# A different hand-over of the last pair of sequences to the router and to the first expert tile, in an attention and mixture-of-experts kernel

## The chip, the cores and the metric

The kernel runs on one core of a Trainium2 chip. The metric is the device time of one execution in microseconds (us). Each kernel is timed in several runs, and the median is given with the lowest and the highest. Durations of single instructions come from one execution under the hardware profiler.

## What is computed

Sixteen sequences of 100 tokens with 256 features go through two layers:

```python
x = x + cross_attention(layernorm(x), ctx)      # 16 heads of 16, rotary positions, window of 64 keys back
xf = layernorm(x).reshape(1600, 256)
probs = softmax(xf @ router_w.T)                # 8 experts
topk_p, topk_i = top_k(probs, 2); topk_p /= topk_p.sum(-1)
for e in range(8):
    mask = (topk_i == e).any(-1)
    mean_w = (topk_p * (topk_i == e)).sum() / mask.sum()     # one weight for each expert
    out += mask * ((silu(xf @ gate_e.T) * (xf @ up_e.T)) @ down_e.T) * mean_w
x = x + out
```

An expert works only on the tokens that chose it. Its products are made from numbers split in a high part (TensorE's rounded fp32 format, fp32r) and a low part (what is left), three products for one: high by high, low by high, high by low.

## The kernel before, in words

**Attention.** The 16 sequences are worked off as NPAIR = 8 pairs. Each engine has its own hand-written program with a loop `for i in range(-1, NPAIR + 2)` over pairs and inside it `for n in range(8)` over quarters of heads. At (i, n) it does pair i's attention, prepares pair i + 1, finishes pair i - 1 (output projection, residual) and routes pair i - 2. The order of instructions on an engine is the order in this text; semaphores (`s_...`) tie the engines together. Nothing is planned at run time.

**Routing of a pair i - 2.** VectorE: `residual` (L997) adds the attention output to x and takes mean and variance (`norm_stats`, s_var2). POOL: `inverse_deviation` (L1235) makes rstd2. VectorE: `rows_write` (L1006) writes the normalized rows and their token numbers into `xrow` (s_xr). TensorE: `x2_transpose` (L547) turns them; ACT: `x2_copy` (L772) copies them; TensorE: `route_logits` (L557); VectorE: `choose` (L1016) takes the best of 8, `choose_masks` (L1028) and `choose_counts` (L1037) build `sel`, `chosen` and the running counts `before` (s_ch), `top_differences` (L1077) the difference of the two best logits (s_dl). TensorE: `ranks` (L567) sums how many earlier tokens chose each expert. VectorE: `places` (L1043), `destinations` (L1050) make the row numbers in `slots`, a DRAM array with a region for each expert. POOL: `scatter` (L1267) sends the rows there, four indirect DMAs a pair. ACT: `top_exponentials` (L779); POOL: `weight_sums` (L1249), seven small operations, adds the weights of the experts up (s_wpair).

**The first tile of expert 0.** An expert tile has 448 tokens. Tile 0 does not wait for the last two pairs' scatters. SP loads what is in `slots` into `xin` early (L382), TensorE transposes it into two banks (`early_tile`, L586), and the rows of pairs 6 and 7 that belong to expert 0 are added there by products with a matrix of ones and zeros (`late_rows`, L594). That needs the high and low part of the rows (`rows_high` on ACT, L785; `rows_low` on VectorE, L1061) and the matrix `onehot`: `hot_columns` (L1066) compares the slot numbers with the token's own (`here`), one column block for each sequence. After the last pair TensorE sums the counts (L664) and the weights (L669). `warm` (L581) issues products whose result nobody reads.

**The experts.** In `block` (L709) TensorE runs eight steps f: `hidden` (L681), 12 products for gate and up, and from f = 3 on `project_down` (L695) of step f - 3. At f = 7, before `hidden`, it transposes the next tile out of `xin` (`tile_transpose`, L673). ACT and VectorE follow it in their `step` functions (L873, L1191). In a step VectorE does `gated` (silu times up), waits for ACT's `hidden_high`, does `hidden_low`, and in the first tile of an expert also `weights_low`, which waits for ACT's `weights_high`; these split the next expert's weights.

**The tokens' numbers.** Each row in `xin` carries its token number. `take_ids` (L1177) copies them to `idnext`, once `xin` has landed (s_in), and adds to s_id. There is one `xin`. SP (L405 to L411) loads tile t when tile t's turn of s_xt (transposes of tile t - 1 done) and of s_id (numbers of tile t - 1 taken) has come; both start with a credit of one. Tile 0 is so loaded a second time, whole, after all scatters, for its numbers alone. With e == 0, `take_ids(0)` stands at f == FC - 5 = 3, and `take_ids(t + 1)` at f == FC - 2 = 6:

```python
for f in range(FC):                 # VectorE, L1193
    gated(t, f)
    hidden_low(t, f)
    if split and f < WCH:           # WCH = 6
        weights_low(e, par, f)
    if e == 0 and split and f == FC - 5:
        take_ids(0)
```

## Time and profile before

| what | value |
|---|---|
| median of 3 runs | 486.79 us (485.64 to 487.36) |
| the profiled execution, its own time | 483.92 us |
| its span in the trace | 482.1 us |
| TensorE busy in the span | 446.3 us (93%) |
| VectorE, ACT, POOL busy | 301.0, 272.6, 142.0 us |
| mean granted clock of TensorE | 0.982 |
| expert tiles | 8, one for each expert |

The span is what the trace covers; the own time of that execution is 1.8 us longer. Attention takes about the first 200 us of the span, routing of the last two pairs the next 15, the experts the rest. PE is TensorE, PEld its weight loads, DVE is VectorE, ACT is ScalarE, POOL is GpSimd, SP issues DMAs. PEclk is the granted clock, 1.00 for 2.4 GHz and 0.50 for 1.2 GHz. An idle time in square brackets is the engine's wait ahead of that instruction, with what ended it.

### The profile page before, as it was taken

Reading aid. Unit: us, or ns where it says so; the run is one execution under the profiler, and the core shown is the slowest. Engines: PE = TensorE matmul, PEld = TensorE weight load, DVE = VectorE, ACT = ScalarE, POOL = GpSimd, SP = SyncE. Lnnn points to the kernel's source line nnn. Section 1 sums busy time; section 2 is a strip of 40 time slices with the busy share of each in tenths; the row PEclk is TensorE's granted clock in tenths of the full one; section 3 lists DMA queues with packets and bytes.
Section 4 is the critical chain, followed back from the end, with each engine's and each line's share of the span. In section 5 each row is a group of like instructions: output and inputs, shape, how many; then the busy total and the mean of one; then the engine's idle time right before and its main releaser. Section 6 shows DMA issues by size and latency. Waiting matters only on the chain.

```text
span 482.1 us, 8983 instructions
## 1 busy us (share of the span) xinstructions
PE 446.3 (93%) x2787; PEld 367.9 (76%) x2787; DVE 301.0 (62%) x735; ACT 272.6 (57%) x863; POOL 142.0 (29%) x174
## 2 busy tenths in 40 slices
PE   3898999999999999889999999999999999999980
PEld 2655666757565655569899999999999999999980
DVE  2565769898979878775737647466465473763330
ACT  1286887878788888335445545455464554554230
POOL 5111013544446262673023050140410502205013
PEclk9999999999999999989999999999999999999995
DMA  8173421111202020229956545565465553213002
GB/s 229 41 210 111 175 78 33 39 41 33 67 6 67 8 63 26 84 76 384 300 151 155 180 78 170 166 125 164 111 164 154 89 170 94 27 40 41 0 5 34
DMA packets 24588, 50.48 MB, mean 105 GB/s; under 512 B 5410, under 2 KB 15302, under 8 KB 24394
## 3 DMA queue, kind: packets, MB, share of 16 engines
q10 hardware_dynamic: 7886, 26.44, 17.6%
q1 hardware_dynamic: 10508, 16.47, 11.3%
q0 software_dynamic: 6144, 6.97, 8.8%
q8 instruction: 23, 0.38, 0.3%
q14 instruction: 27, 0.22, 0.2%
HBM read 39.62 MB, written 13.20 MB: 110 GB/s over the span
## 4 chain that ended last, share of the span: by engine, by line
PE 69%; DVE 7%; ACT 7%; DMA 5%; issue 5%; POOL 3%; ACTq 1%; POOLq 0%; SPq 0%; DVEq 0%
PE b_o L703 9%; PE b_small L703 8%; PE b_s L690 7%; PE b_s L692 7%; PE b_s L691 7%; PE b_s L445 6%; ACT probs L831 4%; PE b_pv L468 3%; PE b_proj L523 3%; PE b_pt L454 3%; PE b_pt L690 2%; PE b_pt L692 2%; PE b_pt L691 2%; PE b_proj L499 2%; DMA xin<-slots 2%
## 5 line engine op out<-in xcount | busy, mean ns | idle before, releaser
L831 ACT ACTIVATE probs<-b_s,negmax 100x100 f32<-100x100 f32 x256 | 85.4, 359 | 24.1 <-DVE negmax L1108 16.7
L1320 POOL DMA_INDIRECT out<-y_sb,idnow x32 | 49.7, 1552 | 158.7 <-ACT y_sb L869 151.4
L857 ACT CAST h_hi<-h_sb 128x448 fp32r<-128x448 f32 x64 | 36.3, 567 | 88.1 <-DVE h_sb L1185 88.1
L690 PE MATMUL b_s<-x_hi,w_hi 128*128 128x448 f32 x192 | 71.5, 372 | 0.0
L692 PE MATMUL b_s<-x_hi,w_lo 128*128 128x448 f32 x192 | 70.4, 367 | 0.0
L691 PE MATMUL b_s<-x_lo,w_hi 128*128 128x448 f32 x192 | 70.0, 364 | 0.0
L1086 DVE TENSOR_TENSOR w_lo<-w_raw,w_hi 128x1024 fp32r<-128x1024 f32 x48 | 58.8, 1225 | 13.8 <-ACT w_hi L792 13.4
L1189 DVE TENSOR_TENSOR h_lo<-h_sb,h_hi 128x448 fp32r<-128x448 f32 x64 | 40.0, 625 | 40.5 <-ACT h_hi L857 39.9
L831 ACT ACTIVATION_READ_ACCUMULATOR probs<-b_s,negmax 100x1 f32 x256 | 56.5, 221 | 0.0
L445 PE MATMUL b_s<-kblk,qrot 128*100 128x400 f32 x128 | 53.7, 500 | 0.0
L792 ACT CAST w_hi<-w_raw 128x1024 fp32r<-128x1024 f32 x48 | 50.4, 1050 | 0.0
L1108 DVE TENSOR_REDUCE negmax<-b_s 100x4 f32<-100x400 f32 x64 | 36.2, 566 | 20.6 <-PE b_s L445 20.2
L1185 DVE TENSOR_TENSOR h_sb<-b_s,act 128x448 f32<-128x448 f32 x32 | 19.9, 620 | 43.7 <-PE b_s L692 39.8
L853 ACT ACTIVATE act<-b_s 128x448 f32<-128x448 f32 x64 | 34.4, 538 | 17.4 <-PE b_s L692 17.4
L692 PEld LDWEIGHTS b_s<-x_hi,w_lo 128*128 128x128 f32 x192 | 36.5, 190 | 2.9
L1274 POOL DMA_INDIRECT slots<-xrow,desti x32 | 34.3, 1072 | 14.7 <-issue 7.3
L691 PEld LDWEIGHTS b_s<-x_lo,w_hi 128*128 128x128 f32 x192 | 36.6, 191 | 2.2
L690 PEld LDWEIGHTS b_s<-x_hi,w_hi 128*128 128x128 f32 x192 | 36.6, 191 | 1.9
L454 PEld LDWEIGHTS b_pt<-cst,probs 100*100 100x100 f32 x256 | 26.2, 128 | 14.8 <-issue 14.2
L703 PE MATMUL b_small<-w_lo,h_hi 128*112 128x256 f32 x128 | 35.9, 281 | 0.0
L703 PE MATMUL b_o<-w_hi,h_lo 128*112 128x256 f32 x128 | 35.9, 280 | 0.0
L703 PE MATMUL b_small<-w_hi,h_lo 128*112 128x256 f32 x128 | 35.9, 280 | 0.0
(153 smaller groups left out, 969.5 us busy)
## 6 DMA issues: line engine op xcount, KB each, us to landing
w_raw<-in_ffw ACTq DMA_DIRECT2D x48, 512.0 KB, 3.9
xin<-slots SPq DMA_DIRECT2D x10, 449.8 KB, 4.4
slots<-in_padrows SPq DMA_DIRECT2D x9, 449.8 KB, 4.1
kblk<-krot SPq DMA_DIRECT2D x128, 12.5 KB
out<-x_all SPq DMA_DIRECT2D x8, 200.0 KB
ctx_all<-in_ctxT SPq DMA_DIRECT2D x1, 1200.0 KB, 6.5
x_all<-in_x SPq DMA_DIRECT2D x1, 1200.0 KB
attw<-in_wT ACTq DMA_DIRECT2D x2, 256.0 KB, 3.9
```

Source lines behind the costliest of these rows:

```text
L445: pe.matmul(o, qrot[:, i % 2, 2 * c + b, :], kblk[:, i % 2, c, h:h + QH, b * S:(b + 1) * S], start=False, stop=True).then_inc(s_s, 1)
L454: m = pe.transpose(b_pt[0:S, h * S:(h + 1) * S], probs[:, N % 3, h, :], ident[0:S, 0:S])
L690: pe.matmul(o, wh[:, c, cols], x_hi[:, c, :], start=(c == 0), stop=False)
L691: pe.matmul(o, wh[:, c, cols], x_lo[:, c, :], start=False, stop=False)
L692: m = pe.matmul(o, wl[:, c, cols], x_hi[:, c, :], start=False, stop=(c == DC - 1))
L703: m = pe.matmul(o, left[:, f, g * ROWS:(g + 1) * ROWS], right[:, f, :], start=(f == 0 and k == 0 and g % 2 == 0), stop=(f == FC - 1 and k ...
L792: nc.scalar.copy(w_hi[1 - par][:, cols], w_raw[:, cols]).then_inc(s_whi, 1)
L831: m = nc.scalar.activation(probs[:, N % 3, h, :], b_s[N % 3][0:S, h * S:(h + 1) * S], ACT.Exp, bias=negmax[:, N % 4, h:h + 1], accum_out=p ...
L857: nc.scalar.copy(h_hi[:, f, :], h_sb[:, f % 2, :]).then_inc(s_hhi, 1)
L1086: V.tensor_tensor(w_lo[1 - par][:, cols], w_raw[:, cols], w_hi[1 - par][:, cols], ALU.subtract).then_inc(s_wlo, 1)
L1189: V.tensor_tensor(h_lo[:, f, :], h_sb[:, f % 2, :], h_hi[:, f, :], ALU.subtract).then_inc(s_hlo, 1)
L1320: G.indirect_dma_start(out, bass.IndirectOffsetOnAxis(idnow[:, n:n + 1], 0), y_sb[:, n, :], None, bounds_check=TOK + TILE - 1, oob_is_err= ...
```

## The change

- Last pair: VectorE subtracts the mean from the rows into `xn` (`rows_center`), without the factor rstd. TensorE transposes these instead of the rows in `xrow`. The choice of experts is the same for every positive factor; the difference of the two best logits is multiplied by rstd in `top_differences`.
- Ranks of pair 6 go to bank `b_pt`; `before` is no longer added up for the last pair. TensorE adds the first sequence's counts with a product more in `ranks`, and the total counts from three products into `b_pt`. The wait ahead of them is on s_rkc, `places(6)`.
- Comparisons for `onehot`: pair 6 both, pair 7 the second, on ACT as Relu(1 - |here - slot|); pair 7's first stays on VectorE. `here` is made straight from the bank, ahead of `places`. `places(7)` moves behind `x_low(0)`.
- `rows_low` moves from VectorE to POOL. POOL's last three operations of the last weight sum go; TensorE adds the five parts instead. All four scatters of pair 6 stand behind the last weight sum (before: two ahead of it).
- `x2_copy(7)` stands ahead of `rows_high(7)` on ACT. `x2_transpose(7)` moves ahead of `ranks(6)` on TensorE, and four of the `warm` products around it go.
- `hidden` begins with the two products that need only the tokens' high part, and waits for the low part after them.
- `take_ids(0)` moves from f == FC - 5 to f == FC - 3.

The diff, cut to its core:

```diff
@@ -545,12 +552,16 @@
     def x2_transpose(i):
-        pe.wait_ge(s_xr, i + 1)
+        if i == NPAIR - 1:
+            pe.wait_ge(s_xc, 1)
+        else:
+            pe.wait_ge(s_xr, i + 1)
...
         for b in range(2):
+            rows = xn[:, b] if i == NPAIR - 1 else xrow[:, i % 2, b]
...
                 m = pe.transpose(b_small[:, (2 * b + c) * S:(2 * b + c + 1) * S],
-                                 xrow[:, i % 2, b, c * P:(c + 1) * P], ident[0:S, 0:S])
+                                 rows[:, c * P:(c + 1) * P], ident[0:S, 0:S])
@@ -566,13 +577,25 @@
     def ranks(i):
         pe.wait_ge(s_ch, i + 1)
-        small_free()
-        o = b_small[0:S, 0:2 * E]
+        if i == NPAIR - 2:
+            pe.wait_ge(s_pTc, NQ * NPAIR)
+            o = b_pt[0:S, 0:2 * E]
+        else:
+            small_free()
+            o = b_small[0:S, 0:2 * E]
...
                   start=True, stop=False)
+        if i == NPAIR - 1:
+            pe.matmul(o[:, E:2 * E], ones_bf[0:S, 0:S], chosen[:, 0, :],
+                      start=False, stop=False)
+            pe.matmul(o, ones_bf[0:S, 0:S], before[:, 0:1, :].to_broadcast([S, 2, E]),
+                      start=False, stop=True).then_inc(s_rk, 1)
+            small_use(s_rkc, i + 1)
+            return
...
                   start=False, stop=True).then_inc(s_rk, 1)
-        small_use(s_rkc, i + 1)
+        if i < NPAIR - 2:
+            small_use(s_rkc, i + 1)
@@ -595,7 +618,10 @@
         for b in range(2):
-            pe.wait_ge(s_hot, 2 * (i - NPAIR + 2) + b + 1)
+            if last and b == 0:
+                pe.wait_ge(s_hot, 1)
+            else:
+                pe.wait_ge(s_hotA, 3 if last else b + 1)
@@ -621,16 +647,15 @@
                 warm(3)
+                x2_transpose(NPAIR - 1)
...
                 den_transpose(2 * i - 1)
-            if n == 0 and i == NPAIR + 1:
-                warm(3)
-            if n == 0 and 0 <= i - 2 < NPAIR:
+            if n == 0 and 0 <= i - 2 < NPAIR - 1:
...
             if n == 0 and i == NPAIR + 1:
-                warm(2)
+                warm(1)
@@ -659,15 +684,18 @@
-    pe.wait_ge(s_ch, NPAIR)
-    small_free()
-    pe.matmul(b_small[:, 0:E], ones_bf[0:S, :], before[:, 2, :],
-              start=True, stop=True).then_inc(s_cnt, 1)
+    pe.wait_ge(s_rkc, NPAIR - 1)
+    for k, counts in enumerate((before[:, 0, :], chosen[:, 0, :], chosen[:, 1, :])):
+        m = pe.matmul(b_pt[:, 0:E], ones_bf[0:S, :], counts, start=(k == 0), stop=(k == 2))
+    m.then_inc(s_cnt, 1)
...
     pe.wait_ge(s_wpair, NPAIR)
-    pe.matmul(b_o[:, 0:E], cst[0:S, C_ONE:C_ONE + P], wacc[:, :],
-              start=True, stop=True).then_inc(s_wsum, 1)
+    for k in range(TOPK * 2 + 1):
+        part = wsel[:, k - 1, :] if k else wacc[:, :]
+        m = pe.matmul(b_o[:, 0:E], cst[0:S, C_ONE:C_ONE + P], part,
+                      start=(k == 0), stop=(k == TOPK * 2))
+    m.then_inc(s_wsum, 1)
...
     def tile_transpose(t):
@@ -686,10 +714,12 @@
                 if f == 0 and which == 0:
+                    pe.wait_ge(s_xhi, DC * t + c + 1)
+                pe.matmul(o, wl[:, c, cols], x_hi[:, c, :], start=(c == 0), stop=False)
+                pe.matmul(o, wh[:, c, cols], x_hi[:, c, :], start=False, stop=False)
+                if f == 0 and which == 0:
                     pe.wait_ge(s_xlo, DC * t + c + 1)
-                pe.matmul(o, wh[:, c, cols], x_hi[:, c, :], start=(c == 0), stop=False)
-                pe.matmul(o, wh[:, c, cols], x_lo[:, c, :], start=False, stop=False)
-                m = pe.matmul(o, wl[:, c, cols], x_hi[:, c, :], start=False, stop=(c == DC - 1))
+                m = pe.matmul(o, wh[:, c, cols], x_lo[:, c, :], start=False, stop=(c == DC - 1))
...
     def project_down(par, t, f, groups=range(GRP)):
@@ -781,6 +811,20 @@
         nc.scalar.activation(etop[:, i % 2], delta[:, i % 2], ACT.Exp).then_inc(s_et, 1)
...
+    def near_columns(i, b):
+        last = i == NPAIR - 1
+        a.wait_ge(s_here, 2 if last else 1)
+        if last:
+            a.wait_ge(s_placed6, 1)
+        else:
+            a.wait_ge(s_slot, 16)
+        done = 3 if last else b + 1
+        nc.scalar.activation(onehot[:, b, :], slot_sb[:, :], ACT.Abs, bias=here[:, b:b + 1], scale=-1.0
+                             ).then_inc(s_abs, 1)
+        a.wait_ge(s_abs, done)
+        nc.scalar.activation(onehot[:, b, :], onehot[:, b, :], ACT.Relu, bias=1.0, scale=-1.0
+                             ).then_inc(s_hotA, 1)
...
     def rows_high(i):
@@ -811,10 +855,12 @@
                 rows_high(NPAIR - 2)
+            if n == 0 and 0 <= i - 2 < NPAIR:
+                x2_copy(i - 2)
...
                 rows_high(NPAIR - 1)
-            if n == 0 and 0 <= i - 2 < NPAIR:
-                x2_copy(i - 2)
+                for b in range(2):
+                    near_columns(NPAIR - 2, b)
@@ -843,6 +889,8 @@
+    near_columns(NPAIR - 1, 1)
...
     def x_high(t):
@@ -1003,6 +1051,12 @@
+    def rows_center(i):
+        v.wait_ge(s_var2, i + 1)
+        for b in range(2):
+            ins = V.tensor_scalar(xn[:, b, :], x_all[:, 2 * i + b, :], mv2[:, b, 0:1], None, ALU.subtract)
+        ins.then_inc(s_xc, 1)
...
     def rows_write(i):
@@ -1029,10 +1083,15 @@
         m = sel[:, i]
-        V.tensor_copy(before[:, 0, :], before[:, 2, :])
+        if i < NPAIR - 1:
+            V.tensor_copy(before[:, 0, :], before[:, 2, :])
...
                              ALU.is_equal))
...
+    def last_counts():
+        m = sel[:, NPAIR - 1]
+        V.tensor_tensor(chosen[:, :, :], m[:, 0:2, :], m[:, 2:4, :], ALU.add).then_inc(s_ch, 1)
...
     def choose_counts(i):
@@ -1042,7 +1101,7 @@
     def places(i):
         v.wait_ge(s_rk, i + 1)
-        V.tensor_tensor(place[:, :, :], b_small[0:S, 0:2 * E].rearrange("p (b e) -> p b e", b=2),
+        V.tensor_tensor(place[:, :, :], rank_bank(i)[0:S, 0:2 * E].rearrange("p (b e) -> p b e", b=2),
@@ -1058,27 +1117,33 @@
-    def rows_low(i):
-        v.wait_ge(s_xrh, i - NPAIR + 3)
-        V.tensor_tensor(xr_lo[:, i % 2], xrow[:, i % 2, :, 0:D], xr_hi[:, i % 2], ALU.subtract
-                        ).then_inc(s_xrl, 1)
...
-    def hot_columns(i):
-        link(V.scalar_tensor_tensor(out=here[:, :], in0=place[:, :, 0], scalar=1.0, in1=chosen[:, :, 0],
-                                    op0=ALU.add, op1=ALU.mult))
-        if i == NPAIR - 2:
-            v.wait_ge(s_slot, 16)
-        else:
-            v.wait_ge(s_placed6, 1)
-        for b in range(2):
-            V.tensor_tensor(onehot[:, b, :], slot_sb[:, :], bc(here[:, b:b + 1], [S, TILE]), ALU.is_equal
-                            ).then_inc(s_hot, 1)
+    def here_columns(i):
+        v.wait_ge(s_rk, i + 1)
+        if i == NPAIR - 1:
+            v.wait_ge(s_ch, NPAIR)
+            v.wait_ge(s_hotA, 2)
+        V.scalar_tensor_tensor(out=here[:, :],
+                               in0=rank_bank(i)[0:S, 0:2 * E].rearrange("p (b e) -> p b e", b=2)[:, :, 0],
+                               scalar=1.0, in1=chosen[:, :, 0], op0=ALU.add, op1=ALU.mult
+                               ).then_inc(s_here, 1)
...
+    def hot_column():
+        v.wait_ge(s_here, 2)
+        v.wait_ge(s_placed6, 1)
+        V.tensor_tensor(onehot[:, 0, :], slot_sb[:, :], bc(here[:, 0:1], [S, TILE]), ALU.is_equal
+                        ).then_inc(s_hot, 1)
...
     def top_differences(i):
...
             v.wait_ge(s_et, i - 1)
-        V.tensor_tensor(delta[:, i % 2].rearrange("p k b -> p b k"), top[:, i, :, 0:TOPK],
-                        bc(top[:, i, :, 0:1], [S, 2, TOPK]), ALU.subtract).then_inc(s_dl, 1)
+        if i < NPAIR - 1:
+            V.tensor_tensor(delta[:, i % 2].rearrange("p k b -> p b k"), top[:, i, :, 0:TOPK],
+                            bc(top[:, i, :, 0:1], [S, 2, TOPK]), ALU.subtract).then_inc(s_dl, 1)
+            return
+        for b in range(2):
+            ins = V.tensor_scalar(delta[:, i % 2, :, b], top[:, i, b, 0:TOPK], top[:, i, b, 0:1],
+                                  rstd2[:, b:b + 1], ALU.subtract, ALU.mult)
+        ins.then_inc(s_dl, 1)
...
     def weights_low(e, par, k):
@@ -1114,13 +1179,11 @@
                 weights_low(-1, 1, i - 3)
-            if n == 1 and i == NPAIR:
-                rows_low(NPAIR - 2)
             if n == 0 and i == NPAIR + 1:
+                here_columns(NPAIR - 2)
                 places(NPAIR - 2)
-                hot_columns(NPAIR - 2)
                 destinations(NPAIR - 2)
-                rows_low(NPAIR - 1)
+                V.tensor_copy(before[:, 0, :], before[:, 2, :])
@@ -1129,8 +1192,11 @@
                 residual(i - 1)
-            if n == 3 and 0 <= i - 2 < NPAIR:
+                rows_center(i - 1)
+            if n == 3 and 0 <= i - 2 < NPAIR - 1:
                 choose_counts(i - 2)
+            if n == 3 and i == NPAIR + 1:
+                last_counts()
@@ -1154,10 +1220,10 @@
-    places(NPAIR - 1)
-    hot_columns(NPAIR - 1)
+    here_columns(NPAIR - 1)
+    hot_column()
     v.wait_ge(s_cnt, 1)
-    link(V.tensor_copy(cnt[:, :], b_small[:, 0:E]))
+    link(V.tensor_copy(cnt[:, :], b_pt[:, 0:E]))
@@ -1195,7 +1261,7 @@
                 weights_low(e, par, f)
-            if e == 0 and split and f == FC - 5:
+            if e == 0 and split and f == FC - 3:
@@ -1214,6 +1280,7 @@
     x_low(0)
+    places(NPAIR - 1)
@@ -1253,9 +1320,13 @@
                                   ALU.mult))
-        pool_link(G.tensor_tensor(wsel[:, :, :], sel[:, i],
+        ins = (G.tensor_tensor(wsel[:, :, :], sel[:, i],
...
                                   .to_broadcast([S, TOPK * 2, E]), ALU.mult))
+        if i == NPAIR - 1:
+            ins.then_inc(s_wpair, 1)
+            return
+        pool_link(ins)
@@ -1263,6 +1334,11 @@
         g.wait_ge(s_wpair, i + 1)
...
+    def rows_low(i):
+        g.wait_ge(s_xrh, i - NPAIR + 3)
+        G.tensor_tensor(xr_lo[:, i % 2], xrow[:, i % 2, :, 0:D], xr_hi[:, i % 2], ALU.subtract
+                        ).then_inc(s_xrl, 1)
...
     def scatter(i, columns=range(TOPK * 2)):
@@ -1292,9 +1368,11 @@
             weight_sums(i - 2)
+        if i == NPAIR - 1:
+            rows_low(NPAIR - 2)
         if i == NPAIR:
-            scatter(i - 2, range(TOPK))
-    scatter(NPAIR - 2, range(TOPK, TOPK * 2))
+            rows_low(NPAIR - 1)
+    scatter(NPAIR - 2)
```

## Rows read from the trace of the kernel before

**Rows 1.** The chain that ended last: start, us, engine (DMA: a transfer) and line

```profile
219.31 0.98 POOL slots L1274
220.60 6.65 DMA slots<-xrow,desti
227.94 5.59 DMA xin<-slots
234.62 5.66 DMA xin<-slots
```

**Rows 2.** Timeline of TensorE in expert 0, and its last transposes

```profile
214.98 0.84 PE L690 MATMUL b_s<-x_hi,w_hi 128*128 128x448 f32 x1
...
240.32 0.60 PE L677 MATMUL b_proj<-cst,xin 112*128 112x112 f32 x4 [0.75 <-DMA xin<-slots]
...
467.50 0.55 PE L677 MATMUL b_pv<-cst,xin 112*128 112x112 f32 x4
```

**Rows 3.** Timeline of VectorE in expert 0: start, us, line, op, [idle before <-releaser]

```profile
219.57 0.62 DVE L1185 TENSOR_TENSOR h_sb<-b_s,act 128x448 f32<-128x448 f32 x1 [3.90 <-issue]
...
221.77 1.23 DVE L1086 TENSOR_TENSOR w_lo<-w_raw,w_hi 128x1024 fp32r<-128x1024 f32 x1 [0.32 <-issue]
...
233.55 0.17 DVE L1179 COPY idnext<-xin 112x4 int32<-112x4 int32 x1 [0.52 <-DMA xin<-slots]
```

**Rows 4.** The tile xin: its loads, from issue to landing

```profile
DMA to landing us min/median/max: 3.3/4.4/5.7
```

**Rows 5.** Timeline of VectorE in the front, 202 to 210

```profile
202.40 0.25 DVE L932 BATCH_NORM_AGGREGATE mv<-stats 100x2 f32<-100x6 f32 x2
...
203.85 0.15 DVE L1011 COPY xrow<-rows_sb 100x1 int32<-100x1 int32 x1 [0.68 <-POOL rstd L1242]
...
205.03 1.20 DVE L1074 TENSOR_TENSOR onehot<-slot_sb,here 100x448 fp32r<-100x448 f32 x2
...
206.80 0.68 DVE L1063 TENSOR_TENSOR xr_lo<-xrow,xr_hi 100x512 fp32r<-100x512 f32 x1
207.40 0.16 DVE L1018 COPY logits<-b_small 100x16 f32<-100x16 f32 x1
...
209.29 0.16 DVE L1041 TENSOR_TENSOR before<-before,chosen 100x8 bf16<-100x8 bf16 x1
```

**Rows 6.** Timeline of TensorE in the front, 204 to 214

```profile
204.94 0.53 PE L552 MATMUL b_small<-cst,xrow 100*128 100x100 f32 x4 [0.99 <-DVE place L1045]
...
206.15 0.84 PE L562 MATMUL b_small<-rw_sb,xn2T 128*100 128x8 f32 x8 [0.34 <-ACT xn2T L776]
...
212.76 0.57 PE L601 MATMUL b_pv<-onehot,xr_lo 100*128 100x448 f32 x1
213.45 0.59 PE L669 MATMUL b_o<-wacc,cst 100*128 100x8 f32 x2
213.90 1.55 PE L583 MATMUL b_s<-mask_bf,ident_bf 100*100 100x400 bf16 x4
```

**Rows 7.** Timeline of ACT: a table load, and a pass over 448 elements

```profile
213.92 1.28 ACT L901 ACT_TABLE_LOAD   x1
...
220.22 0.57 ACT L857 CAST h_hi<-h_sb 128x448 fp32r<-128x448 f32 x1 [1.96 <-DVE h_sb L1185]
```

**Rows 8.** Timeline of POOL: the last pair's weight sums

```profile
210.21 0.67 POOL L1252 TENSOR_TENSOR esum<-etop 100x2 f32<-100x2 f32 x1
...
212.30 0.24 POOL L1256 TENSOR_TENSOR wsel<-sel,wtop 100x32 f32<-100x32 f32 x1
```

**Rows 9.** Line 1286: an addition of 100x512 elements on POOL

```profile
L1286 POOL TENSOR_TENSOR x_all<-x_all,biasrow x8: 1267/1268/1412, 13.1 to 159.3; 100x512 f32<-100x512 f32 x8
```

**Rows 10.** Windows: stretch, its us, busy time of each engine, PEclk, DMA, GB/s

```profile
212.00:214.00 2.00, 1.89 (x8) 1.21 (x7) 1.33 (x7) 1.14 (x3) 1.06 (x5) 0.53 0.00 0
218.00:220.00 2.00, 2.00 (x10) 1.83 (x9) 0.43 (x1) 0.27 (x1) 1.68 (x2) 0.77 1.13 413
471.00:472.00 1.00, 0.00 (x0) 0.00 (x0) 0.00 (x0) 0.00 (x0) 0.96 (x1) 0.76 0.77 85
```

More of the change, by code:

```diff
@@ L232, in build, with rank_bank @@
         b_y = [b_o, b_small]
+        def rank_bank(i):
+            return b_pt if i == NPAIR - 2 else b_small
         wq, wk, wv, wo = (attw[:, n] for n in range(4))
@@ L302, in build @@
         s_slot = sem("s_slot")
+        s_xc = sem("s_xc")
+        s_here = sem("s_here")
+        s_abs = sem("s_abs")
+        s_hotA = sem("s_hotA")
         s_early = sem("s_early")
```

## The prediction

> **What bounds the kernel now.** I read the chain that ended last first. After the attention part it passes through a scatter of the last pair, a load of xin that starts when the scatters have landed, and a second load of xin [rows 1]. Only then does it turn to TensorE, which it does not leave until the last output tile. So two things decide when expert 0 is over: when TensorE starts it, and when the second load lands. The TensorE timeline shows both: the first expert product starts at 214.98, the products run without a gap to 239.57, and the transposes of the next tile start at 240.32, after 0.75 us of waiting for xin [rows 2]. Everything behind 240.32 is dense: whatever moves 240.32 moves the end.
>
> The second load (tile 1) is issued by SP after take_ids(0), VectorE's copy of the row numbers out of xin, because there is one xin buffer. VectorE made that copy at 233.55 at the end of its step 3, having waited 0.52 us for the first load [rows 3]; SP issued the second at 234.62 and it landed 5.66 us later, at 240.28 [rows 1].
>
> **Part 1, the row numbers are taken at step 5 instead of 3.** VectorE's steps in expert 0 are paced by the exchange with ACT. gated(0) starts at 219.57 and the last piece of that step, weights_low, ends at 223.00, 3.43 later; the copy at the end of step 3 was ready to go at 233.55 - 0.52 = 233.03; so three steps are 233.03 - 223.00 = 10.03, 3.34 each [rows 3]. The copy will therefore come at G + 5 x 3.34 + 3.43 = G + 20.1, where G is the start of gated(0). From the copy to the landing the old rows give 0.17 (copy), then 234.62 - 233.72 = 0.90 to SP's issue, then 5.66: together 6.73. The load to landing varies from 3.3 to 5.7, median 4.4 [rows 4], and the 0.90 has no lower bound but zero, since SP will have been waiting for long; so 3.5 at the least, 4.6 + 0.45 = 5.1 with the median landing and half the issue gap, and 6.73 at the most. I take 6.1, near the upper end, because this very load ran beside the weight reloads and still will. The transposes of tile 1 then start at G + 26.2, whatever TensorE does: it gets there itself 24.6 us after its first product in the old rows (214.98 to 239.57), some 2 less at full clock, and waits 6 to 7 us. With the old G of 219.57 this gives 245.8, 5.5 later than 240.32. What the move saves, the 0.52 us wait at step 3, lies beside TensorE's work and is worth nothing.
>
> **Part 2, what the front gives back in G.** The old order: statistics done 202.65, rstd on POOL, rows written from 203.85, transposes 204.94, the logits until 206.99, VectorE free for them only at 207.40 [rows 5, 6].
> - Centred rows: two subtractions of some 0.4 us after 202.65 end near 203.4, the transposes end near 204.05. ACT copies after the exponential that it must do first, 204.35 to 204.9 (a pass of 0.57 at most [rows 7]); logits until 205.8. The counts of pair 6 come 0.75 us later than before, which only ranks(6) and POOL see.
> - VectorE is free for the logits later than they come. From 203.85 to 207.48 it did 3.6 us of work; without the two comparisons (1.20) and rows_low (0.68) 1.75 remain [rows 5], now starting at 204.15 behind the centring, plus 0.2 for the extra copies: choose(7) starts near 206.2 instead of 207.40, and, with two small additions less, the chosen experts are ready at 207.8 instead of 209.45.
> - Comparisons on ACT: four passes (absolute value and Relu for each of two columns) at 0.57 each, as the ACT pass over 448 elements took [rows 7], behind rows_high (205.1 to 205.7): 205.7 to 208.1 with small waits on itself. Such a pass is unseen in the old trace: at least 0.3, if ACT did a column in VectorE's 0.6 [rows 5], at most 0.57 + 0.3 of wait; the 0.57 is the nearest, the same engine and width. ranks(7) stands behind late_rows(6) in TensorE's queue, so it waits for ACT and not for VectorE: about 208.95 instead of 209.50. The 1.7 us gained by the router shrinks to 0.55.
> - Last pair: VectorE's one comparison 209.4 to 210.0, ACT's two passes 209.45 to 210.65, so late_rows(7) ends about 211.7 instead of 213.3 [rows 6].
> - The weight sum on TensorE: five fp32 products instead of one. Two passes took from 213.45 to 213.90, where the warm products follow, at the lower clock, so ten take 2.0 to 2.2 there, against about 1.0 at the full one (eight passes, 0.84) [rows 6]. Then four warm products, 1.08 as in the rows (213.90 to 214.98), or 0.7. The first expert product starts at 211.7 + 1.9 + 1.1 = 214.7 at 1.2 GHz, 213.3 at 2.4 GHz.
> - POOL is covered: rows_low(7) is 1.27 (its addition over 512 elements), ends near 208.7, and the four operations that are left (210.21 to 212.54 in the rows) end near 211.0 [rows 8, 9], before TensorE asks at 211.7. Without that cover each late microsecond is one of TensorE's. All eight scatters now stand behind the sums: the last issues at about 211.6 + 7 x 1.29 = 220.6, as before [rows 1], and the first load lands near 233.5, hidden under step 5.
> - The high part first: both high parts and the first low part are there by 213, before TensorE arrives. Nothing, and later tiles have the same products.
>
> **The clock.** The granted clock was 0.5 (1.2 GHz) from about 212.1 to 218.9, after waits of TensorE such as the 0.99 ahead of the transposes [rows 6, 10]. Such waits remain and four warm products go, so I take the same stretch again: first product 214.7, gated(0) 4.6 later as in the rows, G = 219.3. The new stall is longer than any that kept the clock. TensorE's last transposes ended at 468.05 and the grant was down by about 471.5 [rows 2, 10], so it will be down when tile 1 begins. In the old trace dense work from 213.45 ran at half rate until 218.9, 5.4 us, or 2.7 lost; the lower bound is zero. I take 1.7.
>
> **Sum**, against the profiled execution (span 482.1, its time 483.92, 2.87 below the median of 486.79): transposes 219.3 + 26.2 = 245.5, that is +5.2, and clock +1.7: +6.9, or 490.8 on its own scale and **493.7** on the median's, on which my numbers stand. A measurement here tells 0.3% (1.5 us) from no change.
>
> **Rivals.**
> - Same late load, but the clock holds through the start (28%). The front is shorter, so dense work may count: product at 213.3, G 2.75 later = 216.05, transposes at 242.2, +1.9, clock after the stall +1.7: +3.6, 490.4. Against it: four warm products fewer. With the least landing, 3.5, it would be no change.
> - Faster (9%): VectorE's step cycle is shorter than 3.34, because it starts on queued work, and the copy comes before 234. Then the gain of Part 2 stays: 1.6 us of front, and up to 2 of clock, 483.5 to 485. It decides at a copy time of 234.0 (240.3 less 6.3); with G at 216 it needs a step of 2.9. The steps before agree with 3.34 each, each piece waits for the other engine, and nothing in the diff changes them.
> - The absolute value or Relu needs another ACT table than Exp (3%). A load took 1.28 [rows 7]; three would lie on the path of late_rows, +3.8 in G: 497.5. No row before shows either function. The Trainium skill (ScalarE: Activation LUTs, Table sets) says that relu and abs are in every set, which would make this nothing; its rules for kernel authors also send relu to VectorE, which speaks against this part of the change.
> - No measurable change (5%): the second load lands in 3.3 and is issued at once, with the clock held.
>
> **How the numbers follow.** The likeliest (55%) with its bounds is +3 to +9; with the rival of a held clock at its middle the range is +2 to +9.5: **488.8 to 496.3**. Slower 0.86, the two late-load cases and the table; same 0.05; faster 0.09.
>
> **What would show it.** Right: idnext first copied near 239.5 directly behind the sixth weights_low; SP's second load of xin near 240; TensorE's transposes behind 6 us or more of waiting for xin; a granted clock of 0.5 behind them; ranks(7) behind late_rows(6) near 209. Wrong: a copy before 236, a wait for xin under 3 us, ranks at 208 or before, a table load between two exponentials.

## The result and the profile after

The kernel after took 495.29 us (median of 4 runs, 493.49 to 497.43) against 487.08 (4 runs) for the kernel before: the ratio is 1.0175, with a 95% interval of 1.0138 to 1.0212. The profiled execution took 493.49 with a span of 491.7, against 483.92 and 482.1.

The page of the kernel after, span and part 1:

```profile
span 491.7 us, 9001 instructions
PE 445.5 (91%) x2794; PEld 368.6 (75%) x2794; DVE 299.1 (61%) x731; ACT 276.2 (56%) x869; POOL 142.8 (29%) x173
```

TensorE is busy as long as before (446.3), so the 9.6 us by which the span is longer are, in the main, not work but waiting. Its timeline (start, us, line, [idle before <-releaser]):

```profile
203.26 0.56 PE L563 MATMUL b_small<-cst,xn 100*128 100x100 f32 x4 [0.65 <-DVE xn L1057]
...
206.74 0.44 PE L627 MATMUL b_proj<-onehot,xr_hi 100*128 100x448 f32 x1 [1.37 <-ACT onehot L826]
...
209.48 0.21 PE L586 MATMUL b_small<-chosen,tri_bf 100*100 100x16 bf16 x1
...
213.76 0.55 PE L627 MATMUL b_pv<-onehot,xr_lo 100*128 100x448 f32 x1
...
215.73 0.51 PE L718 MATMUL b_s<-x_hi,w_lo 128*128 128x448 f32 x1
...
222.45 0.47 PE L718 MATMUL b_s<-x_hi,w_lo 128*128 128x448 f32 x1 [1.59 <-DVE h_sb L1251]
...
248.24 1.01 PE L705 MATMUL b_proj<-cst,xin 112*128 112x112 f32 x4 [6.93 <-DMA xin<-slots]
```

The transposes of tile 1 answer to 240.32 in [rows 2]. TensorE finished what it had at 241.31 and waited 6.93 us for xin. One execution's attention ends a little earlier or later than another's (by up to 2.9 us between the profiled executions here), so I count from the start of the five warm products that follow it, 200.58 before and 200.32 after: the transposes stand at 39.74 before and 47.92 after, 8.2 later. VectorE in the same kernel, which answers to [rows 3, 5]:

```profile
206.93 1.06 DVE L1094 TENSOR_TENSOR chosen<-sel 100x16 bf16<-100x16 f32 x1
...
221.77 0.62 DVE L1251 TENSOR_TENSOR h_sb<-b_s,act 128x448 f32<-128x448 f32 x1 [4.93 <-ACT act L901]
...
240.71 1.22 DVE L1151 TENSOR_TENSOR w_lo<-w_raw,w_hi 128x1024 fp32r<-128x1024 f32 x1 [0.32 <-ACT w_hi L836]
241.85 0.16 DVE L1245 COPY idnext<-xin 112x4 int32<-112x4 int32 x1
```

The copy of the token numbers (`idnext`) stands directly behind the sixth weights_low. Then the load and the clock, in the chain that ended last and in windows (PEclk is the third figure from the end):

```profile
242.91 5.29 DMA xin<-slots
```

```profile
207.00:208.00 1.00, 1.00 (x5) 0.62 (x5) 1.00 (x2) 0.74 (x2) 0.95 (x1) 0.66 0.00 0
214.00:215.00 1.00, 1.00 (x10) 0.96 (x9) 0.72 (x2) 0.80 (x3) 0.69 (x2) 0.93 1.47 354
244.00:245.00 1.00, 0.00 (x0) 0.00 (x0) 0.00 (x0) 0.00 (x0) 0.00 (x0) 0.93 0.76 233
250.00:251.00 1.00, 1.00 (x4) 0.87 (x4) 0.00 (x0) 0.00 (x0) 0.00 (x0) 0.50 0.00 0
251.00:252.00 1.00, 1.00 (x5) 0.90 (x4) 0.00 (x0) 0.00 (x0) 0.00 (x0) 0.66 0.54 74
```

The load left 1.06 us after the copy began and landed 5.29 later. The clock was at 1.2 GHz from about 207.3 to 214.1, and again from 244.9, in TensorE's long wait, to 251.7. The 3.4 us after 248.24 at half rate are 1.7 us of products lost, and that closes the account: 8.2 to the transposes and 1.7 behind them are 9.9, less the 0.3 by which the attention ended earlier, 9.6.

### The profile page after: what moved, and what is told of

It is laid out like the page before. It is cut to its first block, busy times and chain, and to the rows that moved or that the text cites. A ratio compares the mean times of both kernels' runs of the same rounds, so it can differ in the third digit from the quotient of the medians.

```text
span 491.7 us, 9001 instructions
## 1 busy us (share of the span) xinstructions
PE 445.5 (91%) x2794; PEld 368.6 (75%) x2794; DVE 299.1 (61%) x731; ACT 276.2 (56%) x869; POOL 142.8 (29%) x173
## 4 chain that ended last, share of the span: by engine, by line
PE 69%; DVE 10%; ACT 7%; issue 4%; DMA 3%; SPq 2%; ACTq 2%; POOL 1%; DVEq 0%; POOLq 0%
PE b_o L733 9%; PE b_small L733 8%; PE b_s L718 7%; PE b_s L722 7%; PE b_s L719 7%; PE b_s L452 5%; ACT probs L877 3%; PE b_pv L475 3%; PE b_pt L461 3%; PE b_pt L718 2%; PE b_pt L722 2%; PE b_pt L719 2%; PE b_s L450 2%; PE b_proj L530 2%; PE b_proj L506 2%
## 5 line engine op out<-in xcount | busy, mean ns | idle before, releaser
L719 PE MATMUL b_s<-x_hi,w_hi 128*128 128x448 f32 x192 | 69.7, 363 | 0.0
```

The source lines that it names most:

```text
L719: pe.matmul(o, wh[:, c, cols], x_hi[:, c, :], start=False, stop=False)
```

## The experiments

Medians are in us, from 4 runs for e2 and 9 to 12 for each of the others. A ratio is to the kernel before, run in turn with it on the same chip (its median there: 486.57 for e1 to e4, 487.03 for e5 to e8, 486.36 for e9 to e12). "From the warm products" is the count of above.

**e1 and e3: the copy earlier in the kernel after.**

```diff
-                    if e == 0 and split and f == FC - 3:
+                    if e == 0 and split and f == FC - 5:      # e1
+                    if e == 0 and split and f == FC - 4:      # e3
```

> Undoes one line of the change: take_ids(0) stands at f == FC - 5 again, all else is as in the kernel after. Theory A (the late copy of the row numbers makes the loss): in the trace of after gated(0) starts at 221.77, so the copy can come at 221.77 + 13.45 = 235.2, the transposes of tile 1 some 6.3 later at 241.5, when TensorE gets there itself (241.2 in after); no low clock behind them. Against 248.24 and 1.7 of clock that is 8.4 us back: 487 on the scale of the medians, a little over the kernel before. Theory B (the loss comes from the front: the clock that falls earlier, the reloads that hold ACT up): the copy moves but the time stays near 495.

> The kernel after with take_ids(0) at f == FC - 4. Theory A: one step of VectorE, 3.34 us, earlier than in after: the copy at 238.5, the transposes at 244.9. If a wait of 3.7 us of TensorE still brings the clock down, 3.3 us less than after, 492; if not, 5 less, 490. Theory B: 495.

**e2: the copy later in the kernel before.**

```diff
-                    if e == 0 and split and f == FC - 5:
+                    if e == 0 and split and f == FC - 3:
```

> The kernel before with one line changed: take_ids(0) at f == FC - 3. Theory A: gated(0) at 219.57 as in before, the copy at 239.7, the transposes of tile 1 at 246.0 behind 6 us or more of waiting, and 1.6 us of low clock behind them: 7.3 over the kernel before, 494.4. Theory B: no difference from before, 487.

Measured: e1 487.33, ratio 1.0021 (0.9991 to 1.0052); e3 491.40, 1.0095 (1.0058 to 1.0131); e2 493.50, 1.0125 (1.0061 to 1.019). One line takes the loss away and one line brings it. VectorE's copy and TensorE's transposes in e2:

```profile
242.21 0.16 DVE L1179 COPY idnext<-xin 112x4 int32<-112x4 int32 x1
```

```profile
248.37 1.01 PE L677 MATMUL b_proj<-cst,xin 112*128 112x112 f32 x4 [6.62 <-DMA xin<-slots]
```

and in e3:

```profile
242.13 0.16 DVE L1245 COPY idnext<-xin 112x4 int32<-112x4 int32 x1
```

```profile
248.28 0.60 PE L705 MATMUL b_proj<-cst,xin 112*128 112x112 f32 x4 [2.89 <-DMA xin<-slots]
```

In e2 TensorE waits 6.62 us where in before it waited 0.75, in e3 2.89. From copy to transposes it is 6.2 in both (6.4 in after). The clock was lost behind the wait in e3 too (0.5 from about 249.0 to 252.4 in its windows), as the dearer of its two cases had it. In e1 there is no wait ahead of the transposes:

```profile
242.78 0.55 PE L705 MATMUL b_proj<-cst,xin 112*128 112x112 f32 x4
```

Theory B falls as the cause of the loss; that e1 is no faster than before says that the rest of the change, as it stands, brings nothing. The front has a part in the size of it all the same: the copy stands 39.18 us from the warm products in e2 and 41.53 in after, because gated(0) does (19.10 and 21.45), and once the copy decides, that delay of 2.35 us goes into the time in full.

**e4: e1 with seven warm products in front of late_rows(6).**

```diff
                     if n == 2 and i == NPAIR + 1:
+                        warm(7)
                         late_rows(NPAIR - 2)
```

> As e1, and seven more warm products ahead of late_rows(6), where TensorE waits 1.37 us for ACT's first column in the kernel after. If the clock that fell at 207.7 instead of 212 is what took the gain of the front, late_rows(7) ends about 2 us earlier than 214.3 and the first expert product starts near 213.7; the copy is then at 233.2 and the transposes at 239.5, some 2 us under e1: 485. If the reloads that ACT issues hold the first silu back, gated(0) moves less than the first product does, and the time stays nearer to e1. If the clock isn't decided there, it is as e1 or 0.5 more.

Measured: 485.38, ratio 0.9971 (0.9943 to 0.9999), 2 under e1; the two intervals just touch. TensorE and VectorE:

```profile
206.79 1.37 PE L606 MATMUL b_s<-mask_bf,ident_bf 100*100 100x400 bf16 x7
208.32 0.44 PE L627 MATMUL b_proj<-onehot,xr_hi 100*128 100x448 f32 x1 [0.16 <-ACT onehot L827]
...
214.85 0.51 PE L719 MATMUL b_s<-x_hi,w_lo 128*128 128x448 f32 x1
...
241.14 0.60 PE L706 MATMUL b_proj<-cst,xin 112*128 112x112 f32 x4 [1.48 <-DMA xin<-slots]
```

```profile
218.49 0.63 DVE L1252 TENSOR_TENSOR h_sb<-b_s,act 128x448 f32<-128x448 f32 x1 [2.39 <-ACT act L902]
...
234.73 0.17 DVE L1246 COPY idnext<-xin 112x4 int32<-112x4 int32 x1 [2.77 <-DMA xin<-slots]
```

The clock was 1.00 in every window from 200 to 256. From the warm products, the first expert product stands at 12.96, against 16.90 in e1, 15.41 in after and 14.40 in before; so with the clock kept the change's front is 1.4 us shorter than before's. Part of that is the clock itself, which before had at half rate from 212.1: with before's own front and the clock at 1.00 throughout, in e11 below, the product stands at 14.05, so the shorter path alone is worth about 1.1. But VectorE now waits 2.77 us for the first load, which leaves only when the scatters have landed, and the transposes stand at 39.25, half a microsecond under before: the scatters set them.

**e7: e1 with all four comparisons on VectorE.**

```diff
                         here_columns(NPAIR - 2)
+                        hot_columns(NPAIR - 2)      # both, VectorE
...
-                        for b in range(2):
-                            near_columns(NPAIR - 2, b)
...
-            near_columns(NPAIR - 1, 1)
```

> e1 with all four comparisons back on VectorE (the others of the change stay). Pair 6's columns would be ready near 206.2 instead of 207.8 in the times of after, so late_rows(6) starts half a microsecond earlier; choose(7) comes 1.2 later, near 206.8, and ranks(7) near 208.5 to 208.7 instead of 209.5. Theory: TensorE's wait for ACT's first column (1.37 us) is what brings the clock down; without it the first expert product starts 1 to 2 us earlier than in e1, 486. Rival: VectorE is now the late one at the last pair, one column more (0.55), and nothing is gained: as e1, 487.3.

Measured: 486.85, ratio 0.9996 (0.9971 to 1.0022), against 487.33 for e1: no difference that this tells. The first expert product came at 16.43 from the warm products (e1: 16.90). The theory's reason was wrong: without ACT's columns TensorE had no wait ahead of late_rows(6), only 0.65 and 0.32 us ahead of the transposes and the logits, and the clock fell all the same, at about 205.7:

```profile
204.00:206.00 2.00, 1.64 (x14) 1.31 (x14) 1.75 (x10) 0.99 (x3) 1.72 (x3) 0.93 0.12 41
206.00:208.00 2.00, 2.00 (x7) 1.83 (x8) 1.86 (x11) 0.21 (x1) 1.61 (x6) 0.50 0.00 0
```

So that wait isn't needed to bring it down. Filling it kept the clock at the hand-over in the traces of e4, e5, e8, e9 and e10, where it had fallen in after, e1 and e3, and the mean granted clock over all runs says the same (median 0.985 in e4, 0.975 in e1). What else decides it is not settled.

**e8: e4 with the old order of the products.**

```diff
                         if f == 0 and which == 0:
-                            pe.wait_ge(s_xhi, DC * t + c + 1)
-                        pe.matmul(o, wl[:, c, cols], x_hi[:, c, :], start=(c == 0), stop=False)
-                        pe.matmul(o, wh[:, c, cols], x_hi[:, c, :], start=False, stop=False)
-                        if f == 0 and which == 0:
                             pe.wait_ge(s_xlo, DC * t + c + 1)
-                        m = pe.matmul(o, wh[:, c, cols], x_lo[:, c, :], start=False, stop=(c == DC - 1))
+                        pe.matmul(o, wh[:, c, cols], x_hi[:, c, :], start=(c == 0), stop=False)
+                        pe.matmul(o, wh[:, c, cols], x_lo[:, c, :], start=False, stop=False)
+                        m = pe.matmul(o, wl[:, c, cols], x_hi[:, c, :], start=False, stop=(c == DC - 1))
```

> e4 with the old order of the products and the wait for the low part ahead of them. My step said that the order is worth nothing, as the low parts are there before TensorE arrives: the same time as e4, 485.4. The rival: in the trace of e4 the first product starts at 214.85 and the second low part was made by VectorE from 213.63 to 214.79, so up to 0.3 could be waited for.

Measured: 486.98, ratio 0.9991 (0.9966 to 1.0017). The first expert product stands at 12.97 from the warm products, in e4 at 12.96: in the front the order is worth nothing. The medians differ by 1.6, with overlapping intervals. e8's profiled execution waited 2.07 us for xin and lost the clock behind it, e4's 1.48 and didn't; whether the order has a part in that is not settled.

**e5 and e9: the load of tile 1 without the copy.** e5 starts from e4 (with the copy at step 5):

```diff
+                if e == 0:
+                    sp.dma_start(ids0[:, :], slots[0:TILE, D:RW]...).then_inc(s_ids0, 16)   # numbers alone
+                    with sp.If(hi - lo - 1), sp.Fori(lo + 1, hi) as t:                      # no second load of tile 0
+                        load(t)
...
+            def take_first_ids():
+                v.wait_ge(s_ids0, 16)
+                V.tensor_copy(idnext[:, :], ids0[:, :]).then_inc(s_id0, 1)
...
-                        take_ids(0)
+                        take_first_ids()
```

> e4 with the loads uncoupled: the token numbers of tile 0 come by a small DMA of their own, so that SP loads tile 1 into xin as soon as the scatters have landed, without waiting for VectorE's copy (which stands at step 5). Theory A (TensorE waits for tile 1 only because of the copy in between): in e4 the scatters let the first load go at 228.80, so tile 1 is there by 235; TensorE, whose first product was at 214.85, gets to the transposes after some 22.6 us of products at full clock, 237.5, and doesn't wait. 241.14 becomes 237.5: 3.6 under e4, 482. The rival: TensorE then waits for VectorE's steps (gated two steps back) and keeps 1 to 2 of it; or the small DMA with 448 pieces of 4 bytes is slow and delays xin: 485.

Measured: 485.10, ratio 0.9957 (0.9927 to 0.9987), where the theory had 482 and its rival 485. SP's small DMA and its load of tile 1, and TensorE:

```profile
229.21 0.66 SPq L425 DMA_DIRECT2D ids<-slots  x1
231.05 0.57 SPq L400 DMA_DIRECT2D slots<-in_padrows  x1
233.85 0.38 SPq L420 DMA_DIRECT2D xin<-slots  x1
```

```profile
240.26 0.60 PE L719 MATMUL b_proj<-cst,xin 112*128 112x112 f32 x4 [1.45 <-DMA xin<-slots]
```

The time is the rival's, and its reasons explain little of it in the trace: TensorE has no wait for VectorE between its first product and the transposes. The small DMA landed 5.2 us after its issue; the load of tile 1 took 6.37, 0.7 more than in before, and whether the small DMA has a part in that was not tried. The load of tile 1 left 4.6 us behind the small DMA, for SP first wrote a tail and read two tile numbers; TensorE waited 1.45. e9 mends that order:

```diff
+            early = [sp.value_load(first[0:1, n:n + 1], ...) for n in range(3)]   # ahead of the wait for the scatters
...
+                if e == 1:
+                    write_tail(2)                                                 # behind the load of tile 1
```

> e5 with SP's order mended: it reads the first tile numbers of experts 0 and 1 ahead of its wait for the scatters, and writes expert 2's tail behind the load of tile 1. In e5 SP issued the small DMA at 229.21 and tile 1 only at 233.85; in between it had a tail write and two reads. Theory: tile 1 goes out near 230.5 and lands by 237, TensorE (there at 238.81 in e5) doesn't wait the 1.45 us: 483.7. The rival: the small DMA's 448 pieces are still on the queues then and the load lands after 239: as e5, 485.

Measured: **481.45**, ratio 0.9905 (0.9871 to 0.9940), with e10 below the fastest of all: 1% under the kernel before and, by the two ratios, 2.7% under the one after. That is 2.2 less than I expected; the load was gone early enough, and TensorE met no wait between its first expert product and the transposes. SP and TensorE:

```profile
229.30 0.66 SPq L429 DMA_DIRECT2D ids<-slots  x1
231.02 0.38 SPq L424 DMA_DIRECT2D xin<-slots  x1
```

```profile
216.11 0.51 PE L738 MATMUL b_s<-x_hi,w_lo 128*128 128x448 f32 x1
...
239.07 0.55 PE L725 MATMUL b_proj<-cst,xin 112*128 112x112 f32 x4
```

There is no wait ahead of the transposes, and they stand at 35.93 from the warm products, 1.6 earlier than in e5 (37.52), as the wait that went would have it. Where the other 2 us between the medians come from is not settled.

**e10: e9 with four of the six reloads behind ACT's first silus.**

```diff
-            for k in range(WCH):
+            for k in range(2):
                 reload(-1, k)
...
                     silu(t, f)
+                    if split and e == 0 and f < 2:
+                        for k in (2 * f + 2, 2 * f + 3):
+                            reload(-1, k)
```

> e9, and ACT issues only two of the six weight reloads ahead of its first silu, the others behind the first two silus. In after, ACT issued the six from 214.35 to 220.1 and its first silu came at 221.12, with the gate bank finished 4.7 us before. If that is a cost of its own, gated(0) comes 0.7 us earlier than in e9 (ACT was held to 218.61 in e5 with the first product at 215.73, where 2.4 us would do), VectorE's steps with it, and as TensorE in e9 is held at f = 2 or 3 at most by those steps, the time falls by 0.3 to 0.7. Rival: nothing, since TensorE doesn't wait for gated any more.

Measured: 481.80, ratio 0.9917 (0.9881 to 0.9953): as e9. gated(0) came 2.76 us behind the first product instead of 3.59, the transposes stand 0.35 us earlier from the warm products (35.58), and the medians don't tell that from nothing. In neither trace does TensorE wait for gated.

**e6, e11 and e12: the same repairs in the kernel before.** e6 has e5's uncoupled load, e11 has e9's and eight more warm products, e12 the warm products alone:

```diff
                     if n == 0 and i == NPAIR + 1:
-                        warm(3)
+                        warm(7)          # e11, e12
...
                         late_rows(NPAIR - 2)
+                        warm(4)          # e11, e12
```

> The kernel before with the same uncoupled loads. Its TensorE waited 0.75 us for tile 1 and no more, since its expert 0 began late; so the uncoupling is worth 0.75 at most: 486.3. If a front that starts TensorE earlier is worth nothing without it and 3 us with it, this run shows it by the difference to e5.

> The kernel before with the uncoupled loads, SP's mended order, and eight more warm products: four ahead of x2_transpose(7), where TensorE waited 0.99 us, four behind late_rows(6), where it waited 0.76. If the clock of the front and the load are all that was to be gained, this is as fast as e9 without any other part of the change: gated(0) 1.9 us earlier by the clock, no wait for tile 1: 484. If the shorter router path counts, e9 is 1 us faster than this.

> The kernel before with the eight warm products of e11 alone. Theory (two things decide, TensorE's arrival and the load of tile 1): the front gets up to 1.9 us faster, but tile 1 comes no earlier, since VectorE already waited 0.52 us for the first load; TensorE waits for it instead: the time falls by less than 0.5, 486.6. The rival, that the clock at the start counts in full: 485.

Measured: e6 484.76, ratio 0.9946 (0.9923 to 0.9968); e11 482.95, 0.9939 (0.9906 to 0.9972); e12 486.10, 1.0002 (0.9980 to 1.0025). e12's time is as its first theory said: the warm products alone give nothing that this tells. Its profiled execution doesn't test the theory's reason, for there the front was no faster: the clock fell all the same (0.5 from about 208.4 to 215.2), the first product stands at 15.58 from the warm products, and ACT's first silu was late. Over its runs the mean granted clock was higher than before's (median 0.985 against 0.979), with no gain in time. e11 has the same warm products and kept the clock at 1.00 from 200 to 256 in its trace, so they don't decide it alone. ACT, VectorE and TensorE in e12:

```profile
218.47 2.38 ACTq L862 DMA_DIRECT2D w_raw<-in_ffw  x3
221.84 0.54 ACT L854 ACTIVATE act<-b_s 128x448 f32<-128x448 f32 x1 [3.93 <-issue]
```

```profile
222.84 0.62 DVE L1186 TENSOR_TENSOR h_sb<-b_s,act 128x448 f32<-128x448 f32 x1 [4.60 <-ACT act L854]
...
236.24 0.16 DVE L1180 COPY idnext<-xin 112x4 int32<-112x4 int32 x1
```

```profile
242.65 0.60 PE L678 MATMUL b_proj<-cst,xin 112*128 112x112 f32 x4 [0.26 <-DMA xin<-slots]
```

e6 gained 2.3 us, 1.5 more than the 0.75 I allowed. In its trace TensorE has no wait ahead of the transposes, and they stand at 39.00 from the warm products, 0.74 under before: that is the 0.75, and no more. The rest stays open. One guess is that in other executions of before gated(0) is later, the copy with it, and the wait longer than 0.75. The one trace of that kind speaks against it: in e12, which has before's loads, gated(0) stands 21.75 us from the warm products (18.99 in before), the copy is late, and TensorE, late itself, waits only 0.26. e9 stands 1.5 us under e11, where I had expected 1, and its first product 1.1 earlier (12.97 against 14.05); the two intervals overlap.

## Why the prediction was right, point by point

The forecast was 493.7 (488.8 to 496.3) and the result 495.29; the likeliest case, late load and low clock, is what happened. All five signs of being right were seen and none of the four of being wrong, but the copy and the load came 2.4 and 2.9 us later than their signs said, for the reason under G.

- **The pace of VectorE and the place of the copy** (G + 20.1): 241.85 - 221.77 = 20.08. The rival of a shorter step is gone; all five steps are 3.34 or 3.35.
- **From the copy to the transposes** (6.1): 6.39 in after, 6.2 in e2 and e3. Near the upper end, as taken; SP's 0.90 us was no leftover of earlier work but came again in full, 242.01 to 242.91, though SP had long been waiting.
- **The clock behind the stall** (1.7): 1.7. The size is luck: it was picked between zero and 2.7. The low rate lasted only 3.4 us behind the transposes, not 5.4, because the clock had gone down at 244.9, within the wait.
- **G, 219.3, is the term that was mis-sized**: 221.77, or 2.5 later, or 2.7 if one counts that this execution's front began 0.26 earlier. With the 0.3 by which the way from the copy to the transposes was longer, it is what separates +6.9 from the +9.6 of the two profiled executions. It has two parts, of opposite sign. The router went as worked out (transposes 203.26, logits taken by VectorE at 205.61, ranks(7) at 209.48 behind late_rows(6), for 203.5, 206.2 and 208.95), but the clock fell at 207.3 instead of 212.1, and here the reasoning failed that took the old stretch over unchanged. So late_rows(7) ran at half rate and ended at 214.3 instead of 211.7, and the first product came at 215.73 instead of 214.7. It rose again earlier, at 214.1, and that should have given all of it back: the first products need 2.76 to gated(0) when nothing else holds it (e10), to 218.5. Then came what no step of mine had: ACT issues six reloads ahead of its first silu, and it was not through with them before 220.10. Another 1.0 us passed until the silu, for which no row has a name; it is 1.0 in e4, e5, e9 and e12 too.

```profile
207.19 0.58 ACT L826 ACTIVATE onehot<-onehot 100x448 fp32r<-100x448 f32 x1
...
216.68 3.42 ACTq L909 DMA_DIRECT2D w_raw<-in_ffw  x3
221.12 0.54 ACT L901 ACTIVATE act<-b_s 128x448 f32<-128x448 f32 x1 [4.73 <-issue]
```

The old rows hid this: there the reloads left from 213.38 to 216.49, before the first gate bank was full. I had taken gated(0)'s 4.6 us from the rows as a matter of the clock alone; the 3.3 us from 218.5 to 221.77 passed on ACT, 2.3 of them behind the reloads and 1.0 in the stretch without a name. In e9 the six took from 214.73 to 218.06 and gated(0) came 3.59 behind the first product. But this is the account of one execution. In e1, with the same front, ACT was through with them at 219.15 and the silu waited for TensorE, whose clock was low for 13.6 us; gated(0) came as late, 21.57 from the warm products against 21.45. So a late G is what after, e1 and e3 (22.20) share, and its cause is not one and the same.
- **What was to be covered**: POOL was covered as said (weight sums done 210.27, last scatter 220.51 for 220.6), and ACT's passes took 0.66 and 0.58, four in 2.44 us, for 2.4.
- **No table load** stands between ACT's absolute values, Relus and exponentials in the trace of after; here the Trainium skill (ScalarE: Activation LUTs, Table sets) and the trace agree. Its rule for kernel authors that relu belongs on VectorE and not on ScalarE was not tested as such: e7 does the comparisons on VectorE in another form (is_equal), and its time can't be told from e1's.

## What to carry to other kernels

When a step is moved to a later place on an engine, ask who waits for its last instruction, not what it costs: here a copy of 0.16 us stood between two loads of the same buffer, and two places further down an engine paced at 3.34 us a step gave TensorE a wait of 6.6 to 6.9 us (e2, after) where it had 0.75. A front that is made faster is cashed only if the transfer that the dense engine meets next comes earlier too; cutting the chain of two loads and mending SP's order took the ratio from 0.9971 (e4) to 0.9905 (e9), where the cut alone gave 0.9957 (e5); in the kernel before the cut gave 0.9946 (e6), more than its trace explains. And the issuing of DMAs counts as work of the engine that issues them, ahead of whatever stands behind them: with four of six moved back, VectorE's first step came 0.8 us sooner behind TensorE's first product (e10 against e9).

## What the runs showed that I had not expected

- A small addition on VectorE (`chosen`, 100x16) took 1.06 us in after, 1.04 to 1.06 in e1, e3, e4, e5, e8, e9 and e10, and 0.14 to 0.18 in other places. Each time it was long, POOL's rows_low (100x512, two inputs) ran over the same stretch, 206.86 to 207.95 in after; in e7, where the two didn't meet, it took 0.18. The Trainium skill (GPSIMD Engine Reference, Specifications) says that POOL shares its SBUF interfaces with VectorE and contends with VectorE instructions that have two SBUF inputs; the rows agree. It cost nothing here, as TensorE was still behind late_rows(6).
- The same six reloads took ACT 3.1 us to issue in before, 5.7 in after, 5.3 in e3 and 5.0 in e12, and 3.1 to 4.1 in the other runs that issue them in a row. Single ones take 0.33. SP's two tail writes (1.95 us for the pair in after) and POOL's scatters are issued in the same stretch; which of them holds ACT up was not tried.
- Where the clock fell at the hand-over, it stayed low for 6.8 us in before, after, e2, e6 and e12, but for 13.6 in e1 and 17.1 in e3 and e7, with late_rows and the first expert products inside. Being busy didn't bring it back soon: in e1 TensorE's last wait of the front ended at 207.79, and the clock was at 1.2 GHz from 208.7 to 222.4. Part of the spread between executions of one kernel may come from there; that was not tried.
